# Both copies of the seventh pair's weights by key ahead of the scaling of the next batch's features, on ScalarE

## The reference, cut to what matters

```python
xn = layernorm(x, ln_x_g, ln_x_b)          # the context
ln = layernorm(latents, ln_l_g, ln_l_b)    # the normalized x of the batch
q = ln @ Wq
kv = jnp.concatenate((xn, ln), axis=1) @ Wkv
k, v = jnp.split(kv, 2, axis=-1)
...
attn = jax.nn.softmax(jnp.where(mask_full, q @ k.T, max_neg))   # per head
out = layernorm((attn @ v) @ Wout, ln_o_g, ln_o_b)
x = x + tanh(g_xattn[0]) * out
```

## Time and profile before

| | |
|---|---|
| median of 3 runs | 4077.01 us (4072.47 to 4078.34) |
| the profiled execution | 4064.86 us, of it span 4063.1 us |
| mean granted TensorE clock | 0.992 of full speed |
| TensorE busy | 3869.5 us (95%), weight loads 2735.7 us (67%) |
| VectorE busy | 2265.2 us (56%) |
| ScalarE busy | 1782.3 us (44%) |
| GpSimd busy | 947.4 us (23%) |

### The profile page before, as it was taken

One profiled execution on the slowest core, in us unless ns is written; L12 is line 12 of the kernel. 1 busy time (PEld: TensorE's weight loads), 2 busy tenths in 40 slices (PEclk: granted clock), 3 DMA queues, 4 the chain that ended last, 5 costly groups with the idle time before them and its releaser, 6 DMA issues. The chain is left out here.

```text
span 4063.1 us, 77036 instructions
## 1 busy us (share of the span) xinstructions
PE 3869.5 (95%) x28219; PEld 2735.7 (67%) x28295; DVE 2265.2 (56%) x7040; ACT 1782.3 (44%) x3844; POOL 947.4 (23%) x1112
## 2 busy tenths in 40 slices
PE   7999999999999999999999889999899999879999
PEld 4666666666666666666666558998666666547885
DVE  4556555665665566465556442122577887634547
ACT  4455455545544554555454221111244545423551
POOL 2212221221222122222212001111112332233550
PEclk9999999999999999999999999999999999989999
DMA  3004133303412330341231015998111221127546
GB/s 122 1 14 126 34 94 125 107 25 121 126 44 85 123 116 16 121 126 52 77 121 64 27 58 213 333 335 286 35 58 57 88 77 63 66 83 226 166 149 222
DMA packets 277213, 445.00 MB, mean 110 GB/s; under 512 B 18737, under 2 KB 236721, under 8 KB 268273
## 3 DMA queue, kind: packets, MB, share of 16 engines
q1 hardware_dynamic: 248432, 381.18, 28.9%
q0 software_dynamic: 18336, 50.62, 3.7%
q10 hardware_dynamic: 10080, 8.28, 0.6%
HBM read 234.10 MB, written 205.91 MB: 108 GB/s over the span
## 5 line engine op out<-in xcount | busy, mean ns | idle before, releaser
L496 POOL TENSOR_SCALAR a_wide_p<-a_wide_p,a_w_inv 128x512 f32<-128x512 f32 x512 | 355.2, 706 | 1442.4 <-DVE a_w_inv L1164 1442.4
L938 ACT ACTIVATE a_wide_p<-a_wide_p,a_row_min 128x512 f32<-128x512 f32 x512 | 363.6, 713 | 120.6 <-DVE a_row_min L1159 120.4
L1234 DVE TENSOR_REDUCE a_q_pad<-ring 128x4 f32<-128x1024 f32 x256 | 302.3, 1218 | 76.3 <-PE ring L720 76.3
L580 PE MATMUL ring<-a_qk 64*128 64x512 f32 x678 | 287.1, 639 | 19.1 <-ACT a_wide_pt L967 12.2
L1159 DVE CUSTOM_DVE_ANT_0 a_wide_p<-ring,a_neg_keys 128x512 f32<-128x512 f32 x339 | 226.9, 688 | 116.4 <-PE ring L580 115.8
L995 ACT ACTIVATE a_probs<-ring 128x1024 f32<-128x1024 f32 x256 | 251.2, 1022 | 83.7 <-PE ring L734 83.7
L1689 PE MATMUL ring<-b_xgt,b_we 128*128 128x128 f32 x2016 | 235.5, 275 | 0.5 <-DVE b_xgt L1879 0.5
L1689 PEld LDWEIGHTS ring<-b_xgt,b_we 128*128 128x128 f32 x2016 | 230.1, 192 | 0.8 <-DVE b_xgt L1879 0.7
L580 PE MATMUL acc<-a_qk 64*128 64x512 f32 x346 | 193.7, 640 | 8.4 <-ACT a_wide_pt L967 5.0
L598 PE MATMUL ring<-ident,a_wide_p 128*128 128x128 f32 x1376 | 194.9, 277 | 6.8 <-ACT a_wide_pt L967 6.8
L2681 ACT ACTIVATE c_probs<-ring 128x1024 f32<-128x1024 f32 x128 | 130.9, 1023 | 153.2 <-PE ring L2413 153.2
(11 more groups left out here) (481 smaller groups left out, 8571.6 us busy)
## 6 DMA issues: line engine op xcount, KB each, us to landing
d_cells<-a_neg_keys SPq DMA_DIRECT2D x66, 2112.0 KB, 18.9
b_we<-in_experts SPq DMA_DIRECT2D x63, 1536.0 KB, 9.1
d_xg<-d_cells SPq DMA_DIRECT2D x159, 132.0 KB, 2.1
d_we<-d_placed_results SPq DMA_DIRECT2D x16, 1024.0 KB, 10.5
a_k_t<-in_ctx_keys SPq DMA_DIRECT2D x16, 512.0 KB, 3.5
a_v_pad<-in_ctx_values SPq DMA_DIRECT2D x16, 512.0 KB, 3.7
c_k_t<-in_ctx_keys SPq DMA_DIRECT2D x16, 512.0 KB, 3.5
c_v_pad<-in_ctx_values SPq DMA_DIRECT2D x16, 512.0 KB, 3.5
```

The costliest lines, as they stand in the source:

```text
L496: ins = pool.tensor_scalar(wide_p[:, h % 4, t, :], wide_p[:, h % 4, t, :], w_inv[:, t, h:h + 1], 1.0, ALU.mult, ALU.mult)
L580: pe.matmul(wbank(name), qk[u % 2][64 * j:64 * j + 64, t * P:(t + 1) * P], qk[u % 2][64 * j:64 * j + 64, 256:768], start=True, stop=True). ...
L938: ins = act.activation(wide_p[:, h % 4, t, :], wide_p[:, h % 4, t, :], ACT.Exp, scale=-1.0, bias=row_min[:, h, t:t + 1], accum_out=row_sum ...
L1234: dve.tensor_reduce(q_pad[:, :, 2 * i:2 * i + 2, HD].rearrange("p t h -> p h t"), s, AX.X, ALU.max, negate=True).then_inc(nr.taken(name), 1)
```

## The change

ScalarE's scaling of the first half of the next batch's features moves from place 33 to place 34, where the second half's already was. So it stands behind both copies of the seventh pair's (u = 6) weights by key, instead of ahead of them.

```diff
                             if on(i + 1):
-                                if p in (33, 34):
-                                    features(i + 1, p - 33)
+                                if p == 34:
+                                    features(i + 1, 0)
+                                    features(i + 1, 1)
```

## The result

| | median | lowest to highest | runs |
|---|---|---|---|
| before | 4078.73 us | 4072.38 to 4082.60 us | 12 |
| after | 4085.34 us | 4076.25 to 4092.71 us | 12 |

The ratio is 1.0017, with a 95% interval of 1.0010 to 1.0025: 6.6 us slower in this comparison, within the 0.2% that the prediction called no change, and within its range. The forecast of 4081 us was 4.0 us above the median shown before; measured are 6.6 us, just above the 2 to 6 us of the forecast's own band. The range, 4072 to 4088 us, is wide enough to hold for no effect at all, so it is the times at the seam, and not the range, that test the mechanism.

The account below looks back on a forecast made before the run. TensorE's in-order queue was taken to set the length of a batch. K 0.26 us later in 15 batches made 3.9 us, lifting the median from 4077.0 to about 4081 us; range 4072 to 4088 us.

Parts of the forecast that it names:

- the forecast's own band: Whole kernel: 0.15 to 0.4 us a batch, 2 to 6 us slower, 4079 to 4083 us, chance 0.69.
- (a): ScalarE's copy for t = 0 comes earlier; TensorE's last four transposes start 0.91 us earlier, their 0.68 us wait gone.
- (b): ScalarE's copy for t = 1 must wait for its transposes, 0.44 us idle that the scalings filled before.
- (c): TensorE's scores of pair 7 start 0.51 us earlier, 0.11 us after the copies that free their banks.
- (d): ScalarE's scalings end 0.45 us later, at 945.50, so TensorE's K starts 0.26 us later.
- the 1.5 us that I had told ahead: Sign in the profile after: K's wait for the scaling up from 0.76 to about 1.5 us.
- (e): Behind K nothing catches up, as ScalarE and VectorE idle there; all of the 0.26 us delay stays on the path.
- The sum of 3.9 us: Whole kernel: 15 batches at 0.26 us each make 3.9 us more.
- The rival of a serialised ScalarE: Scalings lose their overlap behind the waiting copy: 0.71 us a batch, 10.7 us slower, 4087.7 us, chance 0.11.
- The faster rival: TensorE keeps the transposes' 0.91 us, 13.7 us faster, 4063 us; needs scalings ended before 944.4; chance 0.04.
- The 0.68 us wait: TensorE's last four transposes wait 0.68 us for the bank ScalarE's copy for t = 0 frees; predicted to go.
- the estimate from the Trainium skill's figures: ScalarE steps of 0.52 and 0.49 us: scalings end at 945.65, K 0.41 us late, 6.2 us in all.

Follow-up runs that it names:

- the extra scaling: One more 128x256 scaling ahead of n = 1, into an unread tile, added to both kernels: 141.87 against 141.66 us a batch before, 142.30 against 141.84 changed.
- one between: Against the changed kernel, one of the four scalings put between the two copies: 4064.80 us, ratio 0.9990 to the kernel before; again 4063.20 us, 0.9987.
- before + extra: Kernel before plus one more 128x256 scaling on ScalarE ahead of n = 1, into an unread tile: 4069.25 us, ratio 1.0009 to the kernel before.
- changed + extra: Changed kernel plus one more 128x256 scaling on ScalarE ahead of n = 1, into an unread tile: 4076.21 us, ratio 1.0022 to the kernel before.
- The repeats: Changed kernel timed twice more without edit: 4070.07 and 4071.10 us, ratios 1.0006 and 1.0008; the kernel before, again: 4067.01 us, ratio 1.0002.
- the first phase alone: Both kernels with the other three phases left out and x stored after the first: 2438.57 us before, 2441.82 us changed.
- all four scalings first: Against the kernel before, all four scalings moved ahead of both copies (place 33): 4082.34 us, ratio 1.0033.

## Why the prediction was right, point by point

Times are given from the start of the copy of V(6), 941.66 before and 942.39 in the changed kernel.

| step | before | predicted | measured |
|---|---|---|---|
| (a) last four transposes start | 2.05 | 1.14 | 1.21 |
| (b) copy for t = 1 starts | 1.87 | 1.41 | 1.41 |
| (c) first load of the scores | 2.63 | 2.12 | 2.25 |
| (d) first scaling behind both copies | 2.34 | 1.89 | 1.90 |
| (d) last scaling ends | 3.39 | 3.84 | 3.83 |
| (d) K's first load | 3.69 | 3.95 | 3.88 |

(a) and (b) held. The copy for t = 0 is earlier and its wait gone, and the same move opened 0.43 us of idle time on ScalarE, because the second copy's input is not there yet. (a) was 0.07 us early: I had let the last four transposes start when their bank was free, and they stand 0.46 us behind the four ahead of them on TensorE (943.14 to 943.60).

(c) was 0.13 us late: the copies end at 944.40 (ScalarE) and about 944.41 (VectorE), and the load comes at 944.64, 0.23 us behind, where I had taken the 0.11 us that stand behind a copy of ScalarE. The release that counts is VectorE's, as the profile names it. Batch 4 of the same trace has the two copies apart, ScalarE's done at 660.70 and VectorE's at 660.99:

```profile
660.10 0.60 ACT L967 ACTIVATE a_wide_pt<-ring 128x512 f32<-128x512 f32 x1 [0.32 <-PE ring L598]
660.31 0.68 DVE L1170 COPY a_wide_pt<-acc 128x512 f32<-128x512 f32 x1
661.22 0.18 PEld L580 LDWEIGHTS acc<-a_qk 64*128 64x128 f32 x1 [0.95 <-issue]
662.58 0.30 PEld L559 LDWEIGHTS ring<-a_kv_t,shared_w 128*128 128x128 f32 x2 [1.03 <-ACT a_kv_t L928]
```

The load comes 0.23 us behind VectorE's copy again. In batch 0, where VectorE's copy is done 0.4 us ahead of ScalarE's, the load comes 0.11 us behind ScalarE's, as I had taken, and 2.12 us behind the copy of V(6). None of it reached the sum: over the 15 batches the first load of the scores moves between 2.12 and 2.52 us behind the copy of V(6), and K's stays at 3.88 us in every one. That is a second sign, beside the extra scaling, that the scalings and not the scores hold K in the changed kernel.

(d) is the term that was mis-sized. The scalings end where they were expected, but K follows 0.05 us behind (946.22 to 946.27), and I had taken 0.12 us from the first batch. So 0.19 us a batch and not 0.26, 2.8 us and not 3.9. The other kernels in which the scalings hold K agree with 0.05 us: one between, before + extra and changed + extra. With K and the scores off by these amounts, the wait named at K's first load came to 1.3 us and not to the 1.5 us that I had told ahead.

(e) held: the V-to-K distance grew by 0.19 us and the batch by 0.18 to 0.19 us, so nothing behind K catches up.

The sum of 3.9 us for the whole kernel was then 1.1 us too high against the seams, and 2.7 us too low against the first comparison. That the range held in spite of the latter is owed to its width. The repeats, the first phase alone (3.25 us) and the equal seams say that the seams are the cause of about 3 us. The other 3 to 4 us of the first comparison are argued to be scatter behind the seams, by the clocks and the traces above, and not shown to be: the repeats' intervals still hold 1.0015. The first phase alone is 0.4 us above the seams' sum, less than the 1.5 to 3.8 us over which its five runs spread.

The rival of a serialised ScalarE fell: the four scalings take 1.93 us, which is three steps of 0.45 us and a last one of 0.57. The faster rival fell as its condition said: the gain at the transposes ends at K. But it was half right in kind. The 0.68 us wait was real cost, and one between collects a part of it, 0.25 us a batch: it takes the wait away and gives K its scalings no later than before (3.40 us behind the copy of V(6), before 3.39).

By the estimate from the Trainium skill's figures (ScalarE: Activation LUTs, What ACT_TABLE_LOAD costs) the scalings would have ended 0.15 us later than by the rows, at 3.99 us; the trace has it at 3.83 us, with the rows.

## What to carry to other kernels

When two chains meet at one instruction, here the scores' banks and the scaled features at K, putting one of them first pays only until the other is the later one. Write down for each when it is done, and fill the gap that a move opens with a piece of the moved work. The profile may name a releaser where no time is lost: compare the idle time with the same step where nothing is waited for, or add a known piece of work and see how much of it comes out. And when the effect is 0.1% of a kernel, read it from a landmark that repeats 15 times to 0.01 us, as the distance from V(6) to K does here, since the medians of 12 runs moved by more than it.

## What the runs showed of the hardware that I had not expected

The time from a release to TensorE's first load isn't one number. It is 0.05 us from ScalarE's last scaling to K (946.22 to 946.27), 0.11 us from ScalarE's copy to the scores where it is alone the last (and batch 0), and 0.23 us from VectorE's copy to the scores (944.41 to 944.64, 660.99 to 661.22). In batches 3 and 5 of the same trace the last is 0.32 and 0.38 us, and why stays open.

Behind the longest wait of TensorE at the seam its clock was sometimes down. In the kernel with all four scalings first, TensorE waits 1.59 us for the transposes' bank in each seam; in 13 of the 15 it is 6.62 to 6.63 us from V(6) to K, in two 8.28 us. Windows of 11 us of that kernel from 0.53 us before the copy of V(6) on, a usual seam and one of the two:

```profile
948.88:959.88 11.00, 9.27 (x60) 5.63 (x59) 7.64 (x24) 6.41 (x13) 0.96 (x2) 1.00 1.09 341
...
1234.00:1245.00 11.00, 9.27 (x45) 4.73 (x47) 5.98 (x19) 5.31 (x10) 0.71 (x1) 0.84 1.09 341
```

The granted clock is 0.84 in the slow one, a mix of its two levels, and TensorE's timeline there shows the cost at the lower level, right behind the wait: the scores' group takes 1.89 us and the product K 2.88 us, against 1.98 us for K at the higher level. In the other eleven traces of this case, whose longest wait at the seam is 0.93 us (ahead of K in changed + extra), the clock was down at none of the seams; the changed kernel's 15 distances are 5.90 to 5.91 us. What sets the two seams apart from the 13 with the same wait isn't shown, and it is one execution. I had no such cost among the rivals. TensorE in the slow one:

```profile
1237.48 0.66 PE L598 MATMUL acc<-ident,a_wide_p 128*128 128x128 f32 x4 [1.59 <-ACT a_wide_pt L967]
1238.07 1.89 PE L580 MATMUL ring<-a_qk 64*128 64x512 f32 x4
1239.89 2.88 PE L559 MATMUL acc<-a_kv_t,shared_w 128*128 128x512 f32 x4
```
